# Layer 0's adjacency mask: one pass per tile moved from GpSimd to VectorE

## The reference

```python
h = jnp.maximum(_layernorm(x), 0.0)
# layer 0
q, k, v = h @ Wq + bq, h @ Wk + bk, h @ Wv + bv            # split in 12 heads
scores = q k^T / sqrt(32) + beta * adj
scores = where(adj > 0, scores, -9e15)                     # the mask
x = x + softmax(scores) @ v
h = jnp.maximum(_layernorm(x), 0.0)
# layer 1
scores = q k^T / sqrt(384) + 2 * adj                       # no mask
x = x + (softmax(scores) @ v) @ Wo.T + bo
```

## Time and profile before

| | before |
|---|---|
| median of 3 runs (lowest, highest) | 1971.93 us (1971.09, 1972.82) |
| the profiled execution's own time | 1970.11 us |
| its span | 1968.1 us |
| PE busy | 1892.9 us (96%) |
| DVE busy | 1823.9 us (93%) |
| ACT busy | 1609.7 us (82%) |
| POOL busy | 995.1 us (51%) |
| chain that ended last | PE 63%, DVE 30%, issue 3% |
| granted TensorE clock, mean | 0.996 |

### The profile page before, as it was taken

How to read it: one execution, slowest core, us unless ns; L and a number is a source line. 1 busy time by engine, 2 the same in 40 slices (tenths; PEclk the granted TensorE clock), 3 DMA queues, 4 the chain that set the end, 5 groups by cost and what they waited for, 6 DMA issues and landing times.

```text
span 1968.1 us, 50014 instructions
## 1 busy us (share of the span) xinstructions
PE 1892.9 (96%) x18336; PEld 1226.6 (62%) x18336; DVE 1823.9 (93%) x3989; ACT 1609.7 (82%) x4151; POOL 995.1 (51%) x1238
## 2 busy tenths in 40 slices
PE   5999999999999999997999999999999999999998
PEld 3566666666666666665666666666666666666665
DVE  5999999999999999998899999999999999999994
ACT  5898988998989889987887777877787777877785
POOL 6466655556766555564353444344343444344331
PEclk9999999999999999999999999999999999999999
DMA  4888989999899999898787887887787887787774
GB/s 138 198 220 227 226 229 231 238 230 241 225 230 225 231 232 236 230 236 213 206 230 187 222 202 202 206 212 198 201 210 190 220 201 206 202 213 197 202 196 119
DMA packets 104722, 415.91 MB, mean 211 GB/s; under 512 B 27008, under 2 KB 31104, under 8 KB 104480
## 3 DMA queue, kind: packets, MB, share of 16 engines
q1 hardware_dynamic: 77728, 305.24, 64.4%
q0 software_dynamic: 26752, 107.49, 17.2%
HBM read 88.61 MB, written 25.17 MB: 58 GB/s over the span
## 4 chain that ended last, share of the span: by engine, by line
PE 63%; DVE 30%; issue 3%; ACT 1%; DMA 1%; POOL 1%; SPq 0%; DVEq 0%; POOLq 0%
DVE s L408 16%; PE ring L294 15%; PE sc L259 15%; PE out L355 11%; DVE pt L421 11%; PE ring L276 6%; PE ring L323 6%; PE ring L302 5%; PE ring L285 2%; PE ring L325 1%; PE ring L314 1%; DVE stats L468 1%; ACT s L531 1%; DVE nmax L408 1%; DMA bias<-in_adj 1%
## 5 line engine op out<-in xcount | busy, mean ns | idle before, releaser
L531 ACT ACTIVATE s<-s,nmax 128x512 f32<-128x512 f32 x1536 | 1095.9, 727 | 200.2 <-DVE nmax L408 199.5
L408 DVE CUSTOM_DVE_ANT_0 s<-sc,bias 128x512 f32<-128x512 f32 x1536 | 968.0, 686 | 55.3 <-PE sc L259 34.7
L421 DVE STREAM_TRANSPOSE pt<-s 128x2048 f32<-128x2048 f32 x285 | 656.8, 2305 | 0.0
L259 PE MATMUL sc<-k,q 32*128 32x512 f32 x3072 | 439.8, 642 | 49.6 <-DVE nmax L408 42.5
L531 ACT ACTIVATION_READ_ACCUMULATOR s<-s,nmax 128x1 f32 x1536 | 313.3, 204 | 0.0
L355 PE MATMUL out<-pk,v 128*32 128x192 f32 x6080 | 286.5, 329 | 0.0
L355 PEld LDWEIGHTS out<-pk,v 128*32 128x32 f32 x6080 | 178.0, 109 | 135.6 <-issue 98.3
L703 POOL TENSOR_TENSOR v<-v,bvx 128x384 f32<-128x384 f32 x64 | 64.6, 1010 | 369.9 <-ACT v L593 369.9
L302 PE MATMUL ring<-wv,hT 128*128 128x384 f32 x1152 | 247.7, 352 | 0.0
L294 PE MATMUL ring<-hT,wq 128*128 128x512 f32 x864 | 241.9, 412 | 1.7 <-DVE hT L436 1.7
L294 PE MATMUL ring<-hT,wk 128*128 128x512 f32 x864 | 239.8, 416 | 0.0
(11 more groups left out here) (94 smaller groups left out, 1897.8 us busy)
## 6 DMA issues: line engine op xcount, KB each, us to landing
pk<-pt SPq DMA_DIRECT2D x1520, 192.0 KB, 4.6
bias<-in_adj POOLq DMA_DIRECT2D x32, 1024.0 KB, 9.6
res<-in_x POOLq DMA_DIRECT2D x16, 768.0 KB, 4.9
x_between<-res POOLq DMA_DIRECT2D x16, 768.0 KB, 5.4
xin<-x_between POOLq DMA_DIRECT2D x16, 768.0 KB, 6.9
res<-x_between POOLq DMA_DIRECT2D x16, 768.0 KB, 5.3
xin<-in_x POOLq DMA_DIRECT2D x15, 768.0 KB, 8.3
out_x<-res POOLq DMA_DIRECT2D x15, 768.0 KB, 3.8
```

The lines of the kernel that those rows point to most:

```text
L259: mm = nc.tensor.matmul(m.sc[:, j, :], m.q[rows, s % 2, P * t:P * (t + 1)], m.k[rows, s % 2, :], start=True, stop=True)
L408: nc.vector.tensor_tensor_reduce(out=m.s[:, t % 2, j, :], in0=m.sc[:, j, :], in1=m.bias[g % 2][:, t, :], scale=s_scale[layer], scalar=3.0e ...
L421: nc.vector.transpose(out=to, in_=m.s[:, t % 2].rearrange("p j (i a e) -> p (j i) a e", a=QUADS, e=HD)).then_inc(turned, 1)
L531: nc.scalar.activation(tile, tile, ACT.Exp, bias=m.nmax[s % 2][:, t, j:j + 1], scale=-1.0, accum_out=m.sums[s % 2][:, t, j:j + 1]).then_in ...
```

## The change

The first pass, the mask, goes from POOL to DVE, into a new function `mask(g, i)`. It waits for the adjacency's load (tile 0) and for the `bias_done` of the tile before, since there is one `mask` buffer. POOL's `bias(g, i)` now waits for it and does the product and the sum. For graph g+1, DVE makes the masks at the end of its steps 3, 5, 7 and 9 of graph g. POOL's steps for tiles 2 and 3 go from 6 and 8 to 7 and 9. For graph 0 DVE makes tile 0's mask ahead of the first step, and the masks of tiles 1 to 3 right behind the scores of steps 0 to 2.

```diff
-X_STEP, ADJ_STEP, RES_STEP, BIAS_STEPS = 9, (1, 5), (6, 3), (3, 5, 6, 8)
+X_STEP, ADJ_STEP, RES_STEP, BIAS_STEPS = 9, (1, 5), (6, 3), (3, 5, 7, 9)
+
+MASK_STEPS = (3, 5, 7, 9)
...
+            def mask(g, i):
+
+                n = NT * g + i
+                if i == 0:
+                    dve.wait_ge(adj_loaded[0], LOADS * (g + 1))
+                if n:
+                    dve.wait_ge(bias_done, n)
+                nc.vector.tensor_scalar(m.mask[:], m.bias[g % 2][:, i, :], 0.0, masked, ALU.is_le, ALU.mult).then_inc(mask_done, 1)
...
             split_low(0, 2)
+            mask(0, 0)
             for g, c, t in steps():
                 s = DT * g + c
                 scores(g, c, t)
+                if s == 0 and t < NT - 1:
+                    mask(0, t + 1)
...
+                if g + 1 < B and NT * c + t in MASK_STEPS:
+                    mask(g + 1, MASK_STEPS.index(NT * c + t))
                 if (g, c, t) in SPLITS:
...
-                nc.gpsimd.tensor_scalar(m.mask[:], tile, 0.0, masked, ALU.is_le, ALU.mult).then_inc(mask_done, 1)
-                pool.wait_ge(mask_done, 2 * n + 1)
-                nc.gpsimd.tensor_tensor(tile, tile, m.nbeta[:].to_broadcast([P, N]), ALU.mult).then_inc(mask_done, 1)
-                pool.wait_ge(mask_done, 2 * n + 2)
+                pool.wait_ge(mask_done, n + 1)
+                nc.gpsimd.tensor_tensor(tile, tile, m.nbeta[:].to_broadcast([P, N]), ALU.mult).then_inc(bias_scaled, 1)
+                pool.wait_ge(bias_scaled, n + 1)
                 nc.gpsimd.tensor_tensor(tile, tile, m.mask[:], ALU.add).then_inc(bias_done, 1)
```

More of the change, by code:

```diff
@@ L164, in two_layers @@
         stats_done, mv_done, rstd_step, h_done = sem("stats_done"), sem("mv_done"), sem("rstd_step"), sem("h_done")
-        hT_high, mask_done, bias_done = sem("hT_high"), sem("mask_done"), sem("bias_done")
+        hT_high, mask_done, bias_done, bias_scaled = sem("hT_high"), sem("mask_done"), sem("bias_done"), sem("bias_scaled")
         scaled, res_added, bo_added = sem("scaled"), sem("res_added"), sem("bo_added")
```

## The result

The changed kernel takes 1994.01 us (median of 4 runs, 1991.44 to 1996.77) against 1972.38 us before in the same comparison (median of 4 too): a ratio of 1.0111, with a 95% interval from 1.0095 to 1.0126. It is slower, by 21.6 us. The forecast was 1998 us with a range from 1984 to 2010.

A forecast was written before the change was run, and what follows sets the result against it. It took PE and DVE, both nearly full and handing over to each other, as the bound. Steady graphs 19.4 us plus opening 7 gave 26.4 on 1970.1, 1996.5; with 1.8 for the median, 1998 us, range 1984 to 2010.

The forecast's parts named there:

- the steady part: Graphs 1 to 15's masks: 1.86 us more on DVE less 0.57 swallowed, 1.29 us a graph, 19.4 us in 15 graphs.
- the opening: Graph 0's masks pass between DVE and POOL per tile, then DVE waits for the adjacency: 7 us, ends 5 and 10.
- What bounds the kernel: Layer 0: PE (96.7%) and DVE (97.4%) nearly full, handing over to each other; POOL at 65.8% isn't bound.
- The pass at 0.34 us: Each mask on DVE costs 0.34 us, the middle between a 0.07 floor and a score pass's 0.61.
- The 0.57 us that DVE can swallow: Room per graph for more DVE work, from its wait for PE's scores: 537.69 - 537.12 = 0.57 us.
- no wait would be left at step 1: Sign in the changed profile: DVE's wait at step 1, 0.72 us before, is gone, and PE waits more for DVE.
- The meetings with POOL at 0.5 us: Masks at steps 7 and 9 held by POOL passes: a quarter microsecond each, 0.5 us a graph, ends 0 and 2.0.
- The costly mask: Rival: a mask costs DVE as much as a score pass, 0.61 us; 2007 us, with meetings 2014; chance 0.20.
- the free one: Rival: steady masks are free, at most 0.14 us each, no meetings; only the opening left, 1979 us; chance 0.08.
- The late adjacency in steady graphs: Rival: loads 2 us slower make a third to half of graphs wait; some 7 us on top, 2005; chance 0.10.
- The faster case: Rival: DVE waited for POOL's order in the opening; removing three masks gives back 5.8 us, 1966; chance 0.03.

The follow-up runs named there:

- experiment 3: Changed kernel with an extra 384-column DVE pass before each mask of graphs 1 to 15: 2021.7 us, ratio 1.0249.
- experiment 10: Changed kernel with graph 0's masks back on POOL and the later graphs' DVE masks at steps 3, 5, 6, 8: 1980.98 us, ratio 1.0035 to before.
- experiment 6: Changed kernel with only tile 0's mask of graphs 1 to 15 on DVE, at the end of step 3, the rest on POOL: 1975.43 us.
- experiment 9: Kernel of experiment 4 with the masks of tiles 1 and 2 ahead of their step's transpose instead of behind it: 1992.44 us.
- experiment 7: Changed kernel with only tile 3's mask of graphs 1 to 15 on DVE, at the end of step 8, the rest on POOL: 1977.78 us.
- experiment 4: Changed kernel with tiles 2 and 3 at steps 6 and 8 instead of 7 and 9, on DVE and POOL: 1988.44 us, ratio 1.0084.
- experiment 2: Changed kernel with only graph 0's masks on DVE, later ones on POOL at steps 3, 5, 6, 8: 1975.03 us, ratio 1.0011.
- experiment 8: Changed kernel with graph 1's adjacency load issued early, right behind that of its x: 1991.65 us, ratio 1.0098.

## Why the forecast came out as it did

The direction and the range held. The sum was 26.4 us for the profiled execution, which measured 22.6 (1992.7 less 1970.1). It came this near in part by luck: the steady part was forecast 5.7 us too high and the opening 2.6 too low, and 2.0 of those 2.6 had nothing to do with its mechanism. By its terms:

**What bounds the kernel** was read rightly. PE and DVE hand over to each other with little room, POOL's time is worth nothing, and taking 122 us from it bought nothing: experiments 3 and 10 show both sides, the first that further DVE work is paid nearly in full, the second that even well-placed masks cost 8 us.

**The pass at 0.34 us** was right as a duration (0.30 to 0.34 from start to start) and too high as a price. Behind a transpose it adds 0.19 (experiments 6 and 9). The forecast had added it to DVE's line without asking what the instruction in front left idle. The Trainium skill, "VectorE: DVE Perf Modes", section on the perf-mode tiers, has two elements a cycle for it; 0.30 against the 0.61 us of a score pass agrees.

**The 0.57 us that DVE can swallow** was too high, and wrongly placed. It can't be used anywhere in the graph: ahead of PE's stretch nothing is swallowed (experiment 6: 0.19 added, 0.21 paid). In PE's stretch, 0.38 was (experiment 7). For all four masks of experiment 4, three at 0.19 and the one behind `hT` at 0.33 add 0.90; less the 0.55 paid, that leaves 0.35, about the same again. The wrong step is in the floor of DVE's wait. The forecast let PE's scores start at 535.85, the moment DVE was done with the ones before, and take 1.11 + 0.16 us from there to DVE's next pass, 1.27 in all. Measured it is 438.14 - 436.66 = 1.48: 0.14 until PE starts, which was put at nothing, then 1.14, then 0.20 (experiment 4). So the forecast that no wait would be left at step 1 failed too: the median is 0.47 us in the changed kernel and 0.36 in experiments 3 and 4. The errors of this term and the last partly cancel: the forecast had 4 x 0.34 - 0.57 = 0.79 us a graph for free masks, and it was 0.55.

**The meetings with POOL at 0.5 us** a graph were right in place and mechanism, and nearly in size: the masks' 32.0 us are 7.4 more than 64 x 0.385, under 0.5 a graph, and 0.37 of it shows in the distance between loads (experiment 4). Only the masks at steps 7 and 9 are held, and whether they are is decided by some two tenths of a microsecond: at 256.26 the mask came 0.13 before POOL's pass and took 0.38, and at 313.06 POOL came 0.09 earlier and it took 1.22. That the forecast hit this size is partly luck, since its quarter of a microsecond per mask was a choice between 0 and 1.0. A term like this can be forecast as a mean only. The rule in the Trainium skill, "SBUF — State Buffer", section on the two sides, that the one who starts first keeps the shared ports for its whole instruction, agrees with these rows for a mask behind a pass of POOL. In the other order it doesn't fit as well: POOL's `add_bv` of 256.39 began 0.25 us before the mask of 256.26 ended and took only 0.12 longer than usual.

With both, the steady graphs cost 13.7 us (12.8 in 14 graphs and 0.9 in the one before) where 19.4 was forecast. This is the term that was mis-sized: 0.91 us a graph and not 1.29.

**The opening at 7 us** was too low: 9.6. Step by step it was right: 2.7 us by step 3, of what isn't due to a later start (2.2 forecast), and 4.57 of waiting for the adjacency (4.2 forecast). Not in the sum were 2.0 us by which step 0 itself begins late; without them the opening costs 7.6, inside the forecast's 5 to 10. PE's first projection began 0.3 us later (22.70 against 22.44), behind small inputs that landed up to 0.5 later, and then took 4.04 us, where it had taken 2.33:

```profile
22.70 4.04 PE L296 MATMUL ring<-hT,wq 128*128 128x512 f32 x9 [1.46 <-DVE hT L438]
26.58 2.26 PE L296 MATMUL ring<-hT,wk 128*128 128x512 f32 x9
```

```profile
22.44 2.33 PE L294 MATMUL ring<-hT,wq 128*128 128x512 f32 x9 [1.66 <-DVE hT L436]
```

This is TensorE's clock, and the profile's windows hide it. They read 1.00 here in both kernels, but the first entry of the trace's clock record, at full clock (2.4 GHz), stands at 26.45 us after the change and at 20.70 before, and ahead of it a window reads 1.00 for want of an entry. The matmuls agree: ahead of 26.45 they start 0.43 us apart, behind it 0.23, which is what the kernel before shows throughout this projection. The second row, the same nine matmuls for `wk`, takes 2.26 us. PE had begun its work at about the same time in both, 18.45 and 17.99, with twelve transposes that took 2.79 us in either; graph 1's twelve, at a granted clock of 1.00, take 1.63. So both openings start at the lower level (1.2 GHz), and what differs is when the full clock comes.

All twelve profiles fall into two groups that way. In four the record begins between 20.70 and 21.49 and the projection takes 2.33 us; in eight it begins between 25.92 and 28.50 and the projection takes 3.74 to 4.18. The slow eight are six of the seven profiles with graph 0's masks on DVE and two of the five with the opening of before (experiments 6 and 10). The fast case of the seven is experiment 2, with the same opening. So the masks on DVE don't decide it; whether they make the late clock likelier can't be told from twelve profiles, and what sets the moment stays open.

Later in the opening PE's pauses show in the granted clock too, 0.66 in the window from 40 to 45 us and 0.56 from 60 to 65. What that costs wasn't measured by itself; the waits for PE at step 5 in experiments 2 and 8, 1.38 and 1.23 us, may be a part of it.

**The rivals.** The costly mask and the free one are both out: it adds 0.19 to 0.33 us where nothing holds it, in the middle. The late adjacency in steady graphs is out too: of the 15 masks at step 3, two waited for the load, 4.57 us in graph 0 and 0.15 in graph 12. The faster case is out: POOL's order in the opening was nobody's wait, and taking the masks out of it made things later (experiment 2).

## What to carry to other kernels

When two engines are both at 97%, moving work from a third one to either of them is paid in the main, whatever the third one gains; ask where in the cycle the added pass stands, since room was found only in the stretch where the other engine leads. An engine's wait isn't all room: take off it the hand-over in both directions, which left 0.36 of 0.72 us here. The price of an added instruction is the change in the distance between its neighbours' starts, which can be a third less than its own when one of them waits for its own engine. And look at the opening apart: work that runs ahead on an idle engine is free there, and once it is tied to a busy engine's steps it delays also whatever that queue issues next. Before two openings are compared, look at where the clock record begins in each.

## What the runs showed of the hardware

The mask on VectorE, float32, 128x512 from SBUF to SBUF, moves what follows by 0.30 to 0.34 us, and one of 511 columns by 0.30 (0.38 recorded for both); on GpSimd it takes 1.93.

Such a pass of VectorE, with one input, is held by a pass of GpSimd that began before it, for up to 0.85 us, and the reverse hold exists and is short: the six passes of `add_bv` that began 0.12 or 0.13 us behind a mask, such as the one at 256.39, took 1.12 to 1.15 us where 1.01 is usual.

TensorE's first projection of nine matmuls took 2.33 us where the clock record began at full clock before it (20.70 to 21.49 us), and 3.74 to 4.18 where it began only at 25.92 to 28.50. A window's granted clock of 1.00 ahead of the first entry of the record says nothing; the distance between two matmuls' starts, 0.43 or 0.23 us, does.
